# Third layer's experts: rest of the gate times up before the next unit's silu and product, and the router weights in eight parts

## The reference, cut to what matters

```python
weights = _golden_weights(x, Wr, temperature)      # [b, t, 8]
gate = jnp.einsum('btd,edf->betf', x, Wg)          # 256 -> 256, eight experts
up = jnp.einsum('btd,edf->betf', x, Wu)
h = jax.nn.silu(gate) * up
e_out = jnp.einsum('betf,efd->betd', h, Wd)
out = jnp.einsum('bte,betd->btd', weights, e_out)
```

## Time and profile before

| | us |
|---|---|
| median of 3 runs | 865.74 |
| lowest and highest run | 864.33 and 867.16 |
| the profiled execution: span from first to last instruction | 865.1 |
| PE busy in the span | 847.5 (98%) |
| DVE, ACT, POOL busy | 631.1, 472.2, 454.6 |

### The profile page before, as it was taken

The page is one execution under the profiler, slowest core; times in us unless marked ns, Lnnn a source line. Parts: engine busy times, 40 slices in busy tenths (PEclk is TensorE's granted clock), DMA queues, the critical chain, the costliest instruction groups (busy, mean ns, idle before and its releaser), DMA issues.

```text
span 865.1 us, 15659 instructions
## 1 busy us (share of the span) xinstructions
PE 847.5 (98%) x5436; PEld 709.6 (82%) x5436; DVE 631.1 (73%) x1275; ACT 472.2 (55%) x944; POOL 454.6 (53%) x316
## 2 busy tenths in 40 slices
PE   8999999999999999999999999999999999999998
PEld 7888888888855899999998878878888887886688
DVE  6898989898987765664656869577667695345767
ACT  3666666666654565656643375732353335357743
POOL 6676767676623646565666021049808225708820
PEclk9999999999999999999999999999999999999999
DMA  8101010101006275456212150011111010030001
GB/s 328 42 19 36 18 36 18 36 18 36 1 1 258 98 241 187 169 169 210 75 42 88 50 206 1 1 50 43 43 36 36 13 62 1 1 146 3 3 2 49
DMA packets 23342, 62.17 MB, mean 72 GB/s; under 512 B 3136, under 2 KB 13632, under 8 KB 20224
## 3 DMA queue, kind: packets, MB, share of 16 engines
q1 hardware_dynamic: 21760, 57.35, 19.5%
q0 software_dynamic: 1536, 4.20, 1.5%
HBM read 50.00 MB, written 8.39 MB: 67 GB/s over the span
## 4 chain that ended last, share of the span: by engine, by line
PE 86%; DVE 7%; POOL 2%; ACT 2%; issue 1%; DMA 1%; SPq 0%; DVEq 0%; ACTq 0%; POOLq 0%
PE banks L102 26%; PE banks L104 25%; PE banks L103 25%; PE banks L1344 3%; PE banks L1330 1%; POOL arenaB L841 1%; DVE banks L1875 1%; POOL arenaC L841 1%; PE banks L999 1%; PE banks L1171 1%; PE banks L933 1%; PE banks L934 1%; DVE arenaC_rounded L1884 1%; PE banks L1013 1%; PE banks L854 1%
## 5 line engine op out<-in xcount | busy, mean ns | idle before, releaser
L2079 ACT ACTIVATE banks<-banks,small 128x512 f32<-128x512 f32 x128 | 84.9, 663 | 79.8 <-DVE small L1480 79.8
L1480 DVE TENSOR_REDUCE small<-banks 128x1 f32<-128x512 f32 x128 | 86.8, 678 | 10.6 <-PE banks L104 10.6
L102 PE MATMUL banks<-xnT_rounded,arenaD_rounded 128*128 128x512 f32 x224 | 89.4, 399 | 0.9 <-POOL arenaC_rounded L721 0.6
L104 PE MATMUL banks<-arenaC_rounded,arenaD_rounded 128*128 128x512 f32 (+1 forms) x256 | 89.6, 350 | 0.0
L103 PE MATMUL banks<-s_tok_rounded,arenaD_rounded 128*128 128x512 f32 x224 | 89.5, 400 | 0.0
L104 PE MATMUL banks<-xnT_rounded,arenaC_rounded 128*128 128x512 f32 x192 | 76.1, 396 | 0.0
L104 PE MATMUL banks<-xnT_rounded,arenaD_rounded 128*128 128x512 f32 x192 | 75.9, 395 | 0.0
L102 PE MATMUL banks<-arenaC_rounded 128*128 128x512 f32 (+1 forms) x192 | 71.4, 372 | 1.1 <-DVE arenaC_rounded L1633 0.6
L1495 DVE SCALAR_TENSOR_TENSOR arenaC<-banks,small,arenaC 128x512 f32<-128x512 f32 x96 | 71.2, 742 | 0.0
L103 PE MATMUL banks<-arenaD_rounded,arenaC_rounded 128*128 128x512 f32 (+1 forms) x192 | 68.5, 357 | 0.0
L707 POOL TENSOR_TENSOR arenaD_rounded<-arenaC,ones 128x512 fp32r<-128x512 f32 x30 | 31.2, 1040 | 55.3 <-DVE arenaC L1495 54.2
(11 more groups left out here) (431 smaller groups left out, 2725.7 us busy)
## 6 DMA issues: line engine op xcount, KB each, us to landing
arenaD<-in_wexp SPq DMA_DIRECT2D x8, 1060.0 KB, 6.3
arenaD<-in_wexp SPq DMA_DIRECT2D x8, 1024.0 KB, 4.8
arenaC<-in_wqkv SPq DMA_DIRECT2D x16, 384.0 KB, 3.1
arenaD<-in_wexp SPq DMA_DIRECT2D x8, 512.0 KB, 3.5
slots<-arenaB SPq DMA_DIRECT2D x1, 2560.0 KB, 10.5
arenaB<-in_sw SPq DMA_DIRECT2D x1, 2084.0 KB, 7.5
arenaC<-in_wo SPq DMA_DIRECT2D x1, 2048.0 KB, 15.9
arenaC<-slots SPq DMA_DIRECT2D x8, 256.0 KB, 3.2
```

Source lines behind the costliest of these rows:

```text
L102: pe.matmul(o, r(lhs[0]), r(rhs[0]), start=start, stop=False)
L104: return pe.matmul(o, r(lhs[1]), r(rhs[0]), start=False, stop=stop)
L1480: dve.tensor_reduce(negmax[:, n % 4:n % 4 + 1], bank[3 + n % 4][:, :], AX.X, ALU.max, negate=True).then_inc(max_done, 1)
L2079: act.activation(prob[r], prob[r], ACT.Exp, bias=negmax[:, r:r + 1], accum_out=rowsum[:, r:r + 1]).then_inc(exp_done, 1)
```

## The change

Four things change in the code.

- **Order of a unit.** DVE runs mult(n) and rest(n), and ACT silu(n) and round(n), so the rest of a unit stands ahead of the next unit's mult and its rounding ahead of the next unit's silu.
- **Router weights.** The chain is cut in eight parts. Parts 0 to 3 (zone, find, mark, find) stand between mult and rest of the first expert's units, parts 4 to 7 (mark, normal, mix, normal) between mult and rest of the second expert's. `gold_done` is still raised behind the first expert's four units.
- **Weights of later experts.** On ACT the two casts of the gate and up weights stand in units 1 and 2 (before: both in unit 1), the cast of the down weights in unit 3 (before: unit 2), all ahead of the unit's round. On DVE `down_rest(e)` moves from the end of the expert's own turn to unit 1 of the next expert, between mult and rest.
- **Loop.** The first two turns of DVE's loop over experts are written out, and the loop starts at pair 1.

```diff
+            def golden_find():
                 link(dve.tensor_reduce(red8[:, 2, :], cand, AX.X, ALU.max))
                 link(dve.tensor_tensor(zone, cand, per(red8[:, 2, :]), ALU.is_equal))
                 link(dve.tensor_tensor(zone, zone, iota, ALU.mult))
                 link(dve.tensor_reduce(red8[:, 3, :], zone, AX.X, ALU.min))
+
+            def golden_mark(k):
+
                 link(dve.tensor_tensor(zone, iota, per(red8[:, 3, :]), ALU.is_equal))
                 link(dve.tensor_tensor(mask2, mask2, zone, ALU.add))
                 link(dve.scalar_tensor_tensor(cand, zone, -4.0, cand, ALU.mult, ALU.add))
                 if k:
                     link(dve.tensor_tensor(fb, fb, mask2, ALU.mult))
+            def golden_normal(v):
+
+                link(dve.tensor_reduce(red8[:, 4, :], v, AX.X, ALU.add))
+                link(dve.tensor_scalar(red8[:, 4, :], red8[:, 4, :], 1e-8, None, ALU.max))
+                link(dve.reciprocal(red8[:, 4, :], red8[:, 4, :]))
+                link(dve.tensor_tensor(v, v, per(red8[:, 4, :]), ALU.mult))
+
+            def golden_mix():
+
                 link(dve.tensor_tensor(fb, fb, per(red8[:, 1, :]), ALU.mult))
                 link(dve.tensor_scalar(red8[:, 1, :], red8[:, 1, :], -1.0, 1.0, ALU.mult, ALU.add))
                 link(dve.tensor_tensor(gw, gw, per(red8[:, 1, :]), ALU.mult))
                 link(dve.tensor_tensor(gw, gw, fb, ALU.add))
...
+            def golden_part(e, n):
+
+                if (e, n) == (0, 0):
+                    golden_zone()
+                elif (e, n) in ((0, 1), (0, 3)):
+                    golden_find()
+                elif (e, n) in ((0, 2), (1, 0)):
+                    golden_mark(e)
+                elif (e, n) == (1, 1):
+                    golden_normal(fb)
+                elif (e, n) == (1, 2):
+                    golden_mix()
+                else:
+                    golden_normal(gw)
...
                     dve.tensor_tensor(v, v, gs[n % 2], ALU.mult).then_inc(gu_done, 1)
-                    if n:
-                        rest_gu(e, q, n - 1)
-                    if n == 3:
-                        rest_gu(e, q, n)
...
                 for n in range(4):
                     mult(0, 0, n)
-                    golden_parts[n]()
+                    golden_part(0, n)
+                    rest_gu(0, 0, n)
                 dve.sem_inc(gold_done, 1)
                 def following(e, q, between=None):
                     for n in range(4):
                         mult(e + 1, 1 - q, n)
+                        if isinstance(e, int) and e == 0:
+                            golden_part(1, n)
+                        elif n == 1:
+                            down_rest(e, q)
+                        rest_gu(e + 1, 1 - q, n)
                         if between and n == 1:
                             between()
                     gateup_rest(e + 2, q)
-                    down_rest(e + 1, 1 - q)
                     add_expert(e, q)
-                with dve.Fori(0, E2 // 2 - 2) as pair:
+                following(0, 0)
+                following(1, 1)
+                with dve.Fori(1, E2 // 2 - 2) as pair:
...
                 for n in range(4):
                     mult(E2 - 1, 1, n)
+                    if n == 1:
+                        down_rest(E2 - 2, 0)
+                    rest_gu(E2 - 1, 1, n)
                 down_rest(E2 - 1, 1)
...
-                def round_gateup(e, q, turn):
+                def round_gateup(e, q, turn, which=range(2)):
...
-                def silu_round(e, q, n):
-                    silu2(e, n)
-                    if n:
-                        round_gu(e, q, n - 1)
-                    if n == 3:
-                        round_gu(e, q, n)
                 for n in range(4):
-                    silu_round(0, 0, n)
+                    silu2(0, n)
+                    round_gu(0, 0, n)
                 def following(e, q, turn):
                     for n in range(4):
-                        silu_round(e + 1, 1 - q, n)
-                        if n == 1:
-                            round_gateup(e + 2, q, turn + 1)
-                        if n == 2:
+                        silu2(e + 1, n)
+                        if n in (1, 2):
+                            round_gateup(e + 2, q, turn + 1, (n - 1,))
+                        if n == 3:
                             round_down(e + 1, 1 - q, turn + q)
+                        round_gu(e + 1, 1 - q, n)
...
                 for n in range(4):
-                    silu_round(E2 - 1, 1, n)
+                    silu2(E2 - 1, n)
                     if n == 2:
                         round_down(E2 - 1, 1, E2 // 2 - 1)
+                    round_gu(E2 - 1, 1, n)
```

More of the change, by code:

```diff
@@ L1748, in golden_zone @@
                 link(dve.memset(mask2, 0.0))
-            def golden_pick(k):
+            def golden_find():
                 link(dve.tensor_reduce(red8[:, 2, :], cand, AX.X, ALU.max))
@@ L1774, in golden_weights @@
                 link(dve.tensor_tensor(gw, gw, fb, ALU.add))
-                normal(gw)
-            golden_parts = [golden_zone, lambda: golden_pick(0), lambda: golden_pick(1), golden_weights]
+            def golden_part(e, n):
[11 more added lines that the diff above has]
+                    golden_normal(gw)
             def residuals(layer, b, between=None):
@@ L2301, in _ @@
                 act.sem_inc(silu2_done, 2)
-                def round_gateup(e, q, turn):
+                def round_gateup(e, q, turn, which=range(2)):
                     act.wait_ge(w2exp_in[q], 16 * turn + 16)
-                    for i in range(2):
+                    for i in which:
                         act.copy(r(wexp2_hi[q][:, i]), wexp2[q][:, i]).then_inc(gateup_rounded, 1)
```

## The result

The changed kernel is slower, as forecast. Its ratio to the kernel before is 1.0085, 95% interval 1.0068 to 1.0101. With the median before at 865.04 us that is 872.4 us, 0.9 above the forecast of 871.5. The median of its own six runs is 873.87 us; one of the six, of 4,054 us, is left out of the ratio.

The account below looks back on a forecast made before the run. PE, busy 98% of the span, was taken as the bound. Stalls of 6.7 us would become 12.6, 5.9 slower: 865.1 + 5.9 = 871.0 profiled, forecast 871.5 us as median; 80% range 859.2 to 874.

Parts of the forecast that it names:

- The reordered unit: Expert stage: rest ahead of the next mult cuts PE's stall loss from 6.7 to 0.9 us, a 5.8 us gain.
- steady stalls: Expert stage: PE's usual waits for the rest of a product, 0.34 us each; all were to go.
- POOL and the small operations: Second expert: small two-input SBUF operations on DVE wait for POOL's current instruction; 12.6 us lost against 6.7 before.
- the open term: Router-weight chain: whether tensor_scalar on DVE also waits for POOL; taken as blocked, though no row showed a long wait.
- The sign I had from L637: POOL's L637 took 0.79 us beside DVE tensor_scalars, 0.69 at least, so tensor_scalar was taken to contend with POOL.
- A: Second expert's router-weight chain: full blocking by POOL, tensor_scalar included; 871.5 us, chance 0.48.
- B: Second expert's router-weight chain: only two-input operations are blocked; 7.2 us lost, 866.2 us, up to 870.8; chance 0.17.
- C: Second expert's router-weight chain: DVE slips in two operations per POOL instruction; 863.4 to 866.4 us, chance 0.13.
- D: Second expert's router-weight chain: small operations not delayed in bulk, all 5.8 us won; 859.9 us, chance 0.22.
- The schedule: Second expert, unit by unit: PE loses 4.2, 2.35, 0 and 5.15 us waiting for DVE's chain beside POOL.
- The base: Whole kernel before: median of the runs taken as 0.6 us above the profiled span of 865.1 us.
- down_rest and the weight casts: Later experts: casts hidden on ACT; `down_rest` in unit 1 costs 0 to 1.6 us, taken as 0.

Follow-up runs that it names:

- gold_late: Changed kernel with the release of POOL's rotary stage moved behind the last golden (router weights) part, second expert, unit 3; ratio to before 0.9942.
- order_only: Changed kernel's order of units and weights, but the whole router-weight chain in the first expert in four parts; ratio to before 0.9960.
- split_only: Kernel before with only the router-weight chain cut in eight over two experts, POOL still released behind the first; ratio to before 1.0140.
- gold_11: Changed kernel with POOL released behind unit 1 of the second expert instead of behind the first expert; ratio to before 1.0034.
- gold_10: Changed kernel with POOL released behind unit 0 of the second expert instead of behind the first expert; ratio to before 1.0039.
- filler: Changed kernel with idle matmuls ahead of the second expert's up product of unit 2 and the third expert's gate products; ratio to before 1.0099.
- filler2: As filler, with 13 more idle matmuls ahead of the second expert's up product of unit 3; ratio to before 1.0079.
- weights_end: gold_late with the weight casts and subtractions back in their places of the kernel before; ratio to before 0.9939.

## Why the prediction was right

- **The reordered unit.** Right. The steady stalls are gone in experts three to eight, and gold_late's stage is 5.5 us shorter than before against 5.8 forecast. The 0.9 us left in the first expert was measured as 0.88.
- **POOL and the small operations.** Right, and the sign came from it. The four kernels that take the overlap away (order_only, gold_late and the two built on it) are faster than before. The one that adds it alone (split_only) is slower.
- **tensor_scalar.** It was the open term, and it is blocked: 2.26 us for 128x8 in the changed kernel, 2.40 in gold_11. The sign I had from L637 was thin, 0.1 us: in the trace before, each of the eight that start beside a pair of L1431 takes 0.78 to 0.79 us, and most of the other eight 0.69. Of the rivals, A held, and B, C and D fell. A slip as in C was seen, but only once in a kernel: in the changed one, gold_10, gold_11, filler and filler2 it is the same product (L1776 in the changed kernel, 0.23), right behind a blocked tensor_scalar.
- **The schedule.** The third expert's gate products start 40.8 us behind the stage's first matmul; my steps put them at 595.6 - 555.1 = 40.5. How the loss is shared out was less exact: 4.7, 1.25 and 3.5 us in the three gaps, against 4.2, 2.35 and 5.15. With the 2.3 us of slow matmuls behind the first gap it is 11.75 against 11.7, since DVE's chain sets the end. POOL began 0.11 us behind the start of the first expert's last rest, not behind its end, and the slow matmuls behind the first gap brought PE later to the second and third.
- **The term that was missing.** The sum had 12.6 us lost and knew no clock. The steps up to the third expert's gate products hold with the slow stretch inside them. Only the second slow stretch, behind the last wait, adds to the time, 1.5 us. That and some 0.4 us of smaller differences make 7.9 us instead of 5.9.
- **The base, and some luck.** I set the median 0.6 us above the profiled span, 865.7. That was the wrong distance: about 2.4 us lie around a span here, and the execution profiled before took longer than the median. The two errors nearly cancel, and the median before came out at 865.04. (My own sum, 871.0 + 0.6, gives 871.6, not 871.5.) That the forecast ends 0.9 us from the 872.4 is in part luck: the base was 0.6 too high and the loss too low, 5.9 against 7.4 by the ratio and 7.9 in the stage.
- **down_rest and the weight casts.** Taken as nothing, and weights_end shows nothing. In the changed kernel the first `down_rest` in unit 1 took 1.80 us beside POOL (600.58, L1877), and PE has no stall there or later.

## What to carry to other kernels

Before a chain of small DVE operations is moved, look at what POOL does at the new place. With two inputs in SBUF, or as a tensor_scalar, each link can cost a whole POOL instruction, however small it is. Cutting such a chain finer doesn't help if the signal that starts POOL stays where it was: move that signal with the end of the chain, and check that POOL has the time to spare (here 23.4 us of waiting further on, of which 14.1 were left). A change made of a gain and a loss is worth taking apart, since here one moved line turns 0.85% slower into 0.6% faster.

## What the runs showed of the hardware

- A tensor_scalar of 128x8 (0.17 us alone) took up to 2.40 us beside a busy POOL. A reciprocal of 128x8 and a reduction of 128x64 beside it kept 0.20 and 0.21. The Trainium skill, page "SBUF — State Buffer", section "Who interferes with whom", says so: tensor_scalar can take the shared pair in a 2-port mode, a reduction never contends on this chip, and outside those modes an instruction with at most one SBUF input doesn't either. The trace agrees in all three.
- POOL can also be the one that waits. In gold_10 a DVE subtraction with two inputs in SBUF (L1877, 128x512) kept its 0.68 us, and POOL's L665 beside it took 2.96 us, 2.4 elsewhere.
- Lower clock behind a wait isn't lost time in itself. After gaps of 4.9 and 3.65 us in the changed kernel, PE's matmuls ran at 0.50 of full speed for 4.9 and 3.4 us. The first stretch ended in another wait and cost nothing, the second cost 1.5 us. In filler2, idle matmuls in the waits kept the clock at 1.00.
- A semaphore raised behind a DVE instruction without a wait for its result started POOL 0.11 us behind that instruction's start, 0.6 us before its end (changed kernel and gold_11).
